# Cached attention on one core: where the value pages, the queries and the own keys are loaded

## The reference

```python
q = _rope(_rmsnorm(x @ Wq.T, q_norm_w), pos)      # 64 x 32 x 32 heads x 128
k = _rope(_rmsnorm(x @ Wk.T, k_norm_w), pos)      # 64 x 32 x  8 heads x 128
kc = k_cache[block_table].reshape(bsz, 512, 8, 128)
vc = v_cache[block_table].reshape(bsz, 512, 8, 128)
k_all, v_all = concatenate([kc, k]), concatenate([vc, v])      # 544 keys
probs = softmax(where(valid, q @ k_all.T * SCALE, -1e30))
o = probs @ v_all
return o @ Wo.T
```

## Time and profile before

| | us |
|---|---|
| median of 3 runs | 3004.65 (3003.25 to 3009.08) |
| the profiled execution, its time | 3007.51 |
| the profiled execution, its span | 3006.0 |
| PE busy in the span | 2975.3 (99%) |
| DVE, ACT, POOL busy in the span | 1804.4, 1551.9, 605.4 |

### The profile page before, as it was taken

The page is one execution under the profiler, slowest core; times in us unless marked ns, Lnnn a source line. Parts: engine busy times, 40 slices in busy tenths (PEclk is TensorE's granted clock), DMA queues, the critical chain, the costliest instruction groups (busy, mean ns, idle before and its releaser), DMA issues.

```text
span 3006.0 us, 89884 instructions
## 1 busy us (share of the span) xinstructions
PE 2975.3 (99%) x36256; PEld 2350.6 (78%) x36256; DVE 1804.4 (60%) x3587; ACT 1551.9 (52%) x2949; POOL 605.4 (20%) x1462
## 2 busy tenths in 40 slices
PE   8999999999999999999999999999999999999999
PEld 7777778767777777777777888888888888888887
DVE  5777779488777777778775444532333343444545
ACT  6666655388787888878784212312333344222221
POOL 0000001355555555555550000000000000300000
PEclk9999999999999999999999999999999999999999
DMA  5333345577777777777676443322333333843311
GB/s 162 106 114 112 98 118 155 167 219 222 215 225 216 224 223 216 220 222 223 218 222 195 126 126 115 95 94 95 103 106 99 113 106 99 245 148 107 109 39 57
DMA packets 506645, 456.28 MB, mean 152 GB/s; under 512 B 33985, under 2 KB 470593, under 8 KB 501698
## 3 DMA queue, kind: packets, MB, share of 16 engines
q1 hardware_dynamic: 470402, 354.41, 39.2%
q0 software_dynamic: 35904, 96.85, 9.9%
HBM read 321.03 MB, written 130.02 MB: 150 GB/s over the span
## 4 chain that ended last, share of the span: by engine, by line
PE 79%; issue 0%; DVE 0%; ACT 0%; DMA 0%; DVEq 0%
PE ps_o L1020 17%; PE ps_scores L1003 12%; PE s_ps L58 8%; PE s_ps L60 8%; PE s_ps L59 8%; PE s_ps_proj L58 5%; PE s_ps_proj L59 5%; PE s_ps_proj L60 5%; PE ps_o L1003 4%; PE s_ps_o L1544 1%; PE s_ps_scores L1520 1%; PE yv_ps L60 1%; PE yv_ps L58 1%; PE yv_ps L59 1%; PE s_ps L1719 0%; PE s_ps L1710 0%
## 5 line engine op out<-in xcount | busy, mean ns | idle before, releaser
L1020 PEld LDWEIGHTS ps_o<-weights_t,v_all 32*128 32x128 f32 x17408 | 502.5, 187 | 60.4 <-issue 34.5
L1020 PE MATMUL ps_o<-weights_t,v_all 32*128 32x128 f32 x17408 | 528.5, 274 | 7.3 <-issue 6.2
L904 ACT ACTIVATE probs<-masked,shift 128x544 f32<-128x544 f32 x512 | 381.6, 745 | 107.2 <-DVE shift L948 91.8
L1003 PE MATMUL ps_scores<-k_slot,q_slot 128*32 128x288 f32 (+1 forms) x6144 | 404.0, 396 | 7.7 <-PEq L98 5.2
L948 DVE CUSTOM_DVE_ANT_0 masked<-ps_scores,reach,scale_now 128x544 f32<-128x544 f32 x384 | 290.4, 756 | 200.6 <-PE ps_scores L1003 200.6
L961 DVE STREAM_TRANSPOSE weights_t<-probs 128x544 f32<-128x544 f32 x512 | 376.7, 739 | 14.6 <-ACT probs L909 1.9
L909 ACT ACTIVATE probs<-probs,inv 128x544 f32<-128x544 f32 x512 | 376.3, 735 | 0.0
L1103 ACT ACTIVATE s_h_hi<-s_h_raw 128x2048 fp32r<-128x2048 f32 x64 | 122.8, 1919 | 486.5 <-PE s_ps L60 483.2
L84 POOL COPY k_slot<-k_pool 128x256 f32 x1024 | 354.7, 406 | 21.2 <-issue 20.7
L1003 PEld LDWEIGHTS ps_scores<-k_slot,q_slot 128*32 128x32 f32 x6144 | 188.6, 110 | 155.0 <-issue 10.2
L58 PE MATMUL s_ps_proj<-y_hi,s_w_hi 128*128 128x512 f32 x640 | 253.1, 395 | 0.0
(11 more groups left out here) (205 smaller groups left out, 5170.7 us busy)
## 6 DMA issues: line engine op xcount, KB each, us to landing
v_all<-vpool_in SPq DMA_DIRECT2D x1024, 128.0 KB, 2.9
qT_scratch<-k_pool SPq DMA_DIRECT2D x32, 1024.0 KB, 5.1
q_slot<-qT_scratch POOLq DMA_DIRECT2D x64, 512.0 KB, 3.7
oT_scratch<-o_t POOLq DMA_DIRECT2D x128, 256.0 KB, 5.1
s_h_raw<-oT_scratch SPq DMA_DIRECT2D x32, 1024.0 KB, 5.7
aT_scratch<-s_o_t SPq DMA_DIRECT2D x32, 1024.0 KB, 5.6
s_h_raw<-aT_scratch SPq DMA_DIRECT2D x32, 1024.0 KB, 5.7
w_raw<-w_in SPq DMA_DIRECT2D x11, 1024.0 KB, 7.6
```

Source lines behind the costliest of these rows:

```text
L904: act.activation(probs[:, k % BUF, :], masked[:, k % 2, :], ACT.Exp, bias=shift[:, k % BUF:k % BUF + 1], scale=-1.0, accum_out=total[:, k ...
L1003: m = pe.matmul(scores_place(n)[q * S:(q + 1) * S, cols], q_slots[j][:, head, r * S:(r + 1) * S], k_slots[j][:, pages, head * PSIZE:(head ...
L1020: m = pe.matmul(ps_o[:, q, 0:GS], v_all[rows, j, t, e * D:(e + 1) * D], weights_t[rows, g, :, t * S:(t + 1) * S], start=t == 0, stop=t == NPP)
```

## The change

The value pages of a sequence are loaded at two moments instead of one. Ahead of the stage all 16 pages of sequence 0 are loaded, and the first 8 of sequence 1 (before: all 16 of both). In step b, for b = 1 to 63, SP reads the numbers of the second 8 pages of sequence b, waits for `pv_done` 2b, issues these 8 transfers into slot b % 2, and then reads the numbers and issues the first 8 pages of sequence b + 1 into the other slot. On POOL, the queries and own keys of b + 2 are loaded behind the copies of the cached keys and behind the wait for `pv_done` 2b, just ahead of the own values.

```diff
         def sync(sp):
-            def load_v_pages(b, slot, half):
+            def pages_of(b, half):
 
                 first = half * NPP // 2
-                page = nc.values_load_multi_w_load_instructions(
+                return nc.values_load_multi_w_load_instructions(
                     c["table"][0:1, bass.ds(b * NPP + first, NPP // 2)], engines=(mybir.EngineType.SP,), min_val=0, max_val=PAGES - 1,
                     skip_runtime_bounds_check_because="the reference's indices lie in the pool")[1]
+
+            def load_v_pages(page, slot, half):
                 for k in range(NPP // 2):
-                    sp.dma_start(v_all[:, slot, first + k, :], a["vpool"][bass.ds(page[k], 1)].rearrange("o p n -> p (o n)")
+                    sp.dma_start(v_all[:, slot, half * NPP // 2 + k, :], a["vpool"][bass.ds(page[k], 1)].rearrange("o p n -> p (o n)")
                                  ).then_inc(v_loaded[slot], 16)
 
-            for b in range(2):
-                for half in range(2):
-                    load_v_pages(b, b, half)
+            load_v_pages(pages_of(0, 0), 0, 0)
+            load_v_pages(pages_of(0, 1), 0, 1)
+            load_v_pages(pages_of(1, 0), 1, 0)
 
             def pair_of(i, first, last):
                 for j in range(2):
                     b = i * 2 + j
-                    if not (first and j == 0) and not (last and j == 1):
+                    if not (first and j == 0):
+                        page = pages_of(b, 1)
                         sp.wait_ge(pv_done, b * 2)
-                        for half in range(2):
-                            load_v_pages(b + 1, 1 - j, half)
+                        load_v_pages(page, j, 1)
+                        if not (last and j == 1):
+                            load_v_pages(pages_of(b + 1, 0), 1 - j, 0)
...
                     if not (last and j >= 2):
                         pool.wait_ge(scores_done, b * HK + HK)
                         pool.sem_inc(pool_passed)
-                        load_qk(b + 2, j % 2)
                         c["gather_k"](pool, b + 2, j % 2)
                     if begun and not (last and j == SEQ - 1):
                         pool.wait_ge(pv_done, b * 2)
                         pool.sem_inc(pool_passed)
+                    if not (last and j >= 2):
+                        load_qk(b + 2, j % 2)
+                    if begun and not (last and j == SEQ - 1):
                         load_v_own(i + (j + 1) // SEQ, (j + 1) % SEQ, (j + 1) % 2)
```

## The result

| | before | after |
|---|---|---|
| median of 4 runs each, us | 3006.86 | 3579.35 |
| all runs, us | 3003.25, 3009.08, 3004.65, 3016.95 | 3584.87, 3572.39, 3573.83, 3586.39 |
| ratio | 1 | 1.1898, 95% interval 1.1856 to 1.194 |
| span of the profiled execution, us | 3006.0 | 3583.3 |

The change makes the kernel 19% slower, by 572 us. The prediction was 3440 us with a range up to 3570: the right sign and the right place, but too small.

What follows compares the result with a forecast made beforehand. PE, with work for 99% of the span, was taken as the bound. Per sequence 4.45 + 0.8 + 1.7 = 6.95, taken as 6.9 us; 63 x 6.9 = 435 us gave about 3440 us, range 3280 to 3570.

Steps and rivals of the forecast that it cites:

- The place and the count: In stage 2, PE waits for the second half's pages before the first value product of sequences 1 to 63: 63 waits.
- stage 3's loads add nothing at the end: At the end of stage 2, the last wait was worth 0 to 4 us beyond the others; nothing was added.
- The wait without queries and keys: PE's wait for the eighth late page: 3.5 us in undisturbed bursts, 5.4 us in disturbed ones, middle 4.45 us.
- T: On PE, the moment a sequence's second value product ends and four scores start; 3.80 us before the next value product.
- Queries and own keys: 640 KB on POOL's queue moving beside the last pages: 0.8 us charged to PE's wait, bounds 0 and 2.0 us.
- the base: The 4.45 us wait for the second half's pages, read from the earlier trace before charging queries and own keys.
- T + 7.3: Predicted landing of the eighth late page in an undisturbed burst, making PE wait 3.5 us.
- The clock: PE's clock falls to 0.50 after each wait in stage 2: 1.7 us a sequence, between 0 and 2.2.
- The heavy rival: Queries and keys paid in full, all bursts disturbed, clock 2.2 us: 9.6 us a sequence, 3610 us; 8%.
- POOL's order costs nothing beyond its share of the burst: On POOL, queries and own keys load behind the copies; none is late, queries being needed 9 us after landing.
- Better overlap: Rival: late pages land 2.2 us after issue, PE waits 2.4 us a sequence, 3155 to 3265 us; 4%.
- no wait: Rival: the late pages land by T + 3.8, so PE never waits for them; 3004 us or slightly lower; 2%.

Runs made afterwards that it cites:

- e4: The change with the second half of the pages issued behind pv_done 2b - 1, one value product sooner: 3045.2 us, ratio 1.0117.
- e9: e4 with POOL's order as in the kernel before the change: 3011.0 us beside 3009.2, ratio 1.0009.
- e1: SP's part of the change alone, queries and own keys issued ahead of the key copies as in the kernel before: 3508.2 us, ratio 1.1659.
- e6: The kernel before the change with a separate semaphore for each half of the pages: 3003.2 us in one run, beside 3008.9.
- e8: e1 with POOL's own values and odd group's store moved behind the even group's store, which waits for the value product: 3316.2 us, ratio 1.1008.
- e5: The change with 26 unread identity products ahead of each first value product from sequence 1 on: 3465.2 us (median of three runs), ratio 1.1524.
- e2: POOL's part of the change alone, SP as in the kernel before: 3051.8 us, ratio 1.0131.

## Why the prediction was wrong in size and right in kind

*The place and the count held.* 63 waits of PE for `v_all`, each in front of a first value product; all other waits of PE in the stage are under 5 us together, but for the one of 5.0 us at its start; the stages behind are unchanged. e4 and e9 show the distance from issue to use as the cause. That stage 3's loads add nothing at the end held too: stage 2 became 576 us longer, and 450.6 us of waits and 63 x 2.09 us of slower products (6.17 against 4.08) are 582.

*The wait without queries and keys, predicted 4.45 us, measured 5.9 (e1).* This is the step that failed most. It added an issue and a landing from the earlier trace rows, 3.3 and 3.7 us. The issue held: the eighth page leaves at T + 4.6 in e1, between the T + 4.0 and T + 5.5 of the forecast. The landing didn't: its median is 5.1 us in e1. The eighth page's landing in the rows was flattered by its neighbours' increments on the same counter; with a counter of its own it is 5.0 us in the same traffic (e6). The trace alone had a hint: the sixteenth page of that sequence, the last on its counter, took 4.3 us, and the prediction put that down to the queries alone. The hint is small, since the median of all sixteenth pages is 4.0 us.

*Queries and own keys, predicted 0.8 us, measured 1.3 (e1 against the change).* Within its bounds of 0 and 2.0, but low. The traffic was also priced as if it began with the queries. The own values and the store, beside the same burst before and after, cost more than queries and keys do: 2.5 us of each landing (e8). They were inside the base, and so were taken for a property of the burst; the T + 7.3 that was read for it is what it reaches with nothing issued beside it (T + 7.2 in e8). That DMA had nothing else to do ahead of T helped nobody, because the traffic that hurts comes behind T.

*The clock, predicted 1.7 us, measured 2.1 in the trace, and a regained 114 us or 1.8 us a sequence in e5, which carries extra products.* The mechanism held in each of the 63 waits. The price was taken from the case of 3.41 us of busy time at 0.50; in the sequences after, PE is busy for 4.4 us of a low stretch on average, as at the stage's start, where the loss was 2.2 us.

*The sum.* 1.4 + 0.5 + 0.4 us too little, times 63, are 145 us; the forecast missed by 139. The heavy rival gave 9.6 us a sequence and 3610 us, for reasons that were partly wrong; it had 8%, and should have had more, since the base was read from records that can only err on the short side.

*POOL's order costs nothing beyond its share of the burst: wrong by itself* (e2, 44 us), though no load in it is late. In the full change this cost isn't seen apart. Of PE's idle pieces without a releaser its stage 2 has one, of 2.4 us; PE waits 7 us in every sequence anyway.

*Better overlap (4%) and no wait (2%)* didn't happen. e8 shows what the former takes: nothing of POOL's queue in the burst's way, and then a wait of 3.4 us, where the rival had 2.4.

*The chances.* Slower was given 0.97, while the cases that it should add up from have 98%; the slip changes nothing here.

## What to carry to other kernels

Before a load is moved nearer to its use, measure how long the whole burst takes to its last byte in the traffic of its new place, with a counter of its own: here the last page is there 7 us behind T left alone, 9.7 beside 384 KB and 11.0 beside 1 MB, against 3.8 us of cover. A load that had 19 us of room says nothing of what it costs with 4. A time to landing is sound only for the last transfer on its counter. And when a fully busy PE is made to wait, add the lower clock behind the wait: here 2 us on top of 7.

## What the hardware showed that was not expected

The two queues don't share evenly. From 1235 us to 1238 us of the trace after, with POOL's megabyte beside the last pages of the burst (DMA queues, columns as in the earlier trace rows):

```profile
q0 software_dynamic: 200, 0.61, 66.4%
q1 hardware_dynamic: 273, 0.24, 25.0%
```

POOL's queue, most of whose packets here have 4 KB and take 159 ns at the median, had 66% of the engines' time, and SP's, with packets of 1 KB at most and 46 ns, 25%. The Trainium skill says that an engine goes round its queues packet by packet ("DMA: Bandwidth & Descriptors", Queues, rings and completion order). The trace doesn't contradict it: the numbers of packets, 200 and 273, are nearer to each other than the times, and the longer packets take the larger share. Whether the page's packet is the profile's, no run here shows.

SP's long issues have a neighbour. In the trace of before, from 700 us to 1500 us, 88 of 810 page issues took over 0.6 us instead of 0.33, and all 88 overlap a 16 KB transfer of the instruction queue; of the other 722, 101 do (counted from the issues of L830 and the packets of that queue). One of them, line L830 in window 849.3:850.5, and the queue's row from 849.3 us to 851.3 us:

```profile
L830 SPq DMA_DIRECT2D v_all<-vpool_in x1: 1780/1780/1780, 849.5 to 849.5; - x1
```

```profile
q8 instruction: 1, 0.02, 4.7%
```

So the disturbed bursts of the earlier trace rows go with instruction transfers, whatever the chain between the two is. And work that keeps an engine from idling can be free: 26 needless products a sequence made the changed kernel 114 us faster in three of its four runs.
